# Expert weights in raw pieces of 512 KB: eight pieces in place of four

## The chip, the cores and the metric

One core of one Trainium2 chip runs the program once; the other cores idle. The metric is the device time of that core in microseconds (us). The kernel before was timed in three runs.

## What is computed

The reference is one graph layer on 625 rows of 1024 float32 numbers: a layer norm, a two-step graph convolution and a linear attention, both added to the input, and then a mixture of experts on the normed sum. The change touches only the last part:

```
logits = xf @ router_w; probs = softmax(logits); topw, topi = top_k(probs, 2)      # 8 experts, 2 for each row
h  = silu(xf @ w1[e])        # 1024 x 1024 for each expert
ye = h @ w2[e]               # 1024 x 1024 for each expert
out = x + sum over e of combine[:, e] * ye + sigmoid(xf @ gate_w) * (silu(gate) * up) @ shared_down
```

All weights are float32. The two tables of the 8 experts are 64 MB together.

## The kernel before, in words

**Split products.** TensorE (PE) multiplies in float32r, so every float32 operand is split into a high part (a rounding copy made by ScalarE, ACT) and a low part (raw minus high, made by VectorE, DVE). Products are summed in PSUM from three passes (high x high, high x low, low x high).

**Jobs.** The weights come as a stream of *jobs*, each a half matrix of 1024 x 512 (2 MB). Jobs 0 to 20 are the dense layers, in two loads of 1 MB each; the last of them is J_D = 20, the first half of shared_down. From J_X = 21 on come the experts, four jobs for each: two halves of w1 (called he0 and he1 here) and two halves of w2 (y0 and y1). After the experts, job J_LOOP is the second half of shared_down. An expert job has four *pieces* of 512 KB (PARTS = 4, two of the eight row blocks of 128 each, PK = 2).

**Buffers.** A piece lands in the raw buffer (w_raw, one job's worth: 16 KB per partition), is copied to w_hi and then subtracted into w_lo. w_hi and w_lo are double: job n uses buffer n % 2, so the split of job n waits until PE has finished job n - 2. The raw buffer is single: SyncE's queue (SP, lines 598 to 615) loads piece s of job n once DVE has made w_lo of piece s of job n - 1 (semaphore lo_done). A load therefore runs one half matrix ahead of the split.

**Order on each engine.** The order is written out by hand and is the same for every expert. PE (lines 2260 to 2292): for each of the two halves of w1, two units "he" of 2 x 8 pairs of matmuls (L2274 high weights against both parts of the rows, L2275 low weights against the high part); transposes of the next expert's gathered rows (L1888); then for each of the two halves of w2 one unit "y" for each tile of up to 128 rows, 8 x 3 matmuls (L1842 to L1844) each. The first unit of a job waits for lo_done piece by piece (weights_in, L1851), the others don't wait for weights. ACT (L1030 to 1066): split_hi of the next job, the activation of two "he" units (copy L1039, silu L1041, he_hi L1043), the same for the second half, then xe (L761), split_hi, y_s (L1055, the copy of a y unit out of PSUM) and its store to DRAM (L1063), split_hi, y_s. DVE (L1762 to 1781) has the counterpart: split_lo (L1092), additions L1772, he_lo L1775, xe L1104.

**Experts.** Seven experts have blocks of fixed size, taken in the order of the sizes 208, 128, 208, 128, 152, 152, 152 rows (called e0 to e6 here); they are unrolled. What is left over goes in blocks of 224 rows through a loop with a register count, which makes one pass in this profile (called e7). On SP the experts and the loop are one loop of "every" passes. GpSimd (POOL, L694 to 723) gathers the rows of the next expert into xg by indirect DMA as soon as the present ones are transposed and split.

**Memory.** Region R1's upper half holds in turn part (the normed rows), gate_s (the silu of the shared gate, read for the last time by L1660, which raises prod_done 8 times), and behind it xg; at the end y_first. Region R2 holds xe and he in high and low parts with a row pitch BS of 256, then y_s and he_s. The tail (L731 to 735, L1789 to 1825) gathers each row's two expert rows, scales them and adds, beside the second half of the shared product on PE.

The lines that set the raw buffer's use before are:

```
raw_part = lambda s: w_raw[s // 2][:, s % 2 * PK:(s % 2 + 1) * PK, :]
sp.wait_ge(lo_done, j * (4 * PARTS) + (count_at(J_X + i, s) - PARTS))     # SP: the piece's split of the job before
act.wait_ge(part_loaded[s], by(16 * (job - J_X + 1), base, 64))           # ACT: this piece has landed
```

Of the kernel before, what the change touches and what calls it, by code (L numbers as in the profile page):

```python
# [5 lines left out]
def gps_layer(nc, x, src, dst, w_self0, w_neigh0, b0, w_self1, w_neigh1, b1,  # L6
# [18 lines left out]
    f32, f32r, f16, b16 = mybir.dt.float32, mybir.dt.float32r, mybir.dt.float16, mybir.dt.bfloat16  # L25
    i32, u32 = mybir.dt.int32, mybir.dt.uint32
    ALU, ACT, AX = mybir.AluOpType, mybir.ActivationFunctionType, mybir.AxisListType


    N, D = x.shape  # L30
# [6 lines left out]
    KF = D // 128  # L37
    HW = D // 2
    HK = KF // 2
    TP, TQ = 628, 640  # L40
# [3 lines left out]
    HH = HW // DH  # L44
    X = router_w.shape[1]
    XP = X + 2
    B, BS = 224, 256
    BROWS = (128, B - 128)
    BC = len(BROWS)
    CAPS = (208, 208, 152, 152, 152, 128, 128)  # L50
    ORDER = (1, 7, 2, 6, 3, 4, 5)
    FIXED = len(ORDER)
# [44 lines left out]
    G, U, Dn = halves(gate), halves(up), halves(down)  # L97
# [71 lines left out]
    LOOP = FIXED  # L169
# [25 lines left out]
    PARTS = 4  # L195
# [28 lines left out]
    with ctx:  # L224
# [3 lines left out]
        def at(name, offset, shape, dt):  # L228
            return nc.alloc_sbuf_tensor_at(name, shape, dt, offset=BASE + offset)
# [23 lines left out]
        x1 = at("x1", R1, [T, NT, D], f32)  # L253
        part = at("part", R1 + R1S // 2, [T, NT, D], f32)
        gate_s = at("gate_s", R1 + R1S // 2, [128, HK, TP], f32)
        xg = at("xg", R1 + R1S // 2 + HK * TP * 4, [128, BC, D], f32)

        TAIL = R2 + RGS
        k_tok = at("k_tok", R2, [T, NT, D], f32)
# [17 lines left out]
        he_lo = at("he_lo", R2 + 3 * XE, [128, KF, BS], f32r)  # L277
        y_s = at("y_s", R2 + 4 * XE, [128, 2, HW], f32)
        he_s = at("he_s", R2 + 4 * XE + 2 * HW * 4, [128, 2, 2, B], f32)
        assert 4 * XE + 2 * HW * 4 + 4 * B * 4 <= PAIR  # L280

        c_f = at("c_f", RC, [T, NT, TP], f32)
        c_lo = at("c_lo", RC, [T, NT, TP], f32r)
# [128 lines left out]
        idx2 = following("idx2", [128, BC], u32, 4)  # L412
        table = following("table", [1, 2, FIXED + MAXB], i32, 4)
        assert BASE + off[0] <= nc.sbuf_usable_end, (BASE + off[0], nc.sbuf_usable_end)
        raw_part = lambda s: w_raw[s // 2][:, s % 2 * PK:(s % 2 + 1) * PK, :]
        off = [o_route]
        lgT = following("lgT", [2 * XP, TP], f32, 4)
        lg = following("lg", [T, NT, XP], f32, 4)
# [44 lines left out]
        ready = [sem(f"psum_ready{n}") for n in range(RING)]  # L463
        free = [sem(f"psum_free{n}") for n in range(RING)]
        w_loaded = [sem(f"w_loaded{n}") for n in range(2)]
        part_loaded = [sem(f"part_loaded{n}") for n in range(PARTS)]
        hi_done = sem("hi_done")
        lo_done = sem("lo_done")
        first_hi_done, first_lo_done, half_normal = sem("first_hi_done"), sem("first_lo_done"), sem("half_normal")
# [76 lines left out]
        def _(sp):  # L546
# [51 lines left out]
                load(job, STREAM[job])  # L598


            sp.wait_ge(table_ready, 1)
            every = sp.value_load(table[0:1, 1, 1:2], min_val=X, max_val=FIXED + MAXB - 1)
            sp.wait_ge(lo_done, count_at(J_D, 1))
            with sp.Fori(0, every) as j:
                expert = sp.value_load(table[0:1, 0, bass.ds(j, 1)], min_val=0, max_val=X - 1)
                for i in range(4):
                    for s in range(PARTS):
                        sp.wait_ge(lo_done, j * (4 * PARTS) + (count_at(J_X + i, s) - PARTS))
                        view = (w1v if i < 2 else w2v)[:, bass.ds(expert, 1), s * PK:(s + 1) * PK,
                                                       (i % 2) * HW:(i % 2 + 1) * HW]  # L610
                        sp.dma_start(raw_part(s), view.rearrange("p e k n -> p (e k) n")).then_inc(part_loaded[s], 16)

            for s in range(PARTS):
                sp.wait_ge(lo_done, every * (4 * PARTS) + (count_at(J_X, s) - PARTS))
                sp.dma_start(raw_part(s), Dn[1][:, s * PK:(s + 1) * PK, :]).then_inc(part_loaded[s], 16)
            for n, (i, c0, c1) in enumerate(OUT_PARTS):
                sp.wait_ge(out_ready, n + 1)
                p0, p1 = row_pieces(i)[0]
# [120 lines left out]
        def _(act):  # L739
# [5 lines left out]
            def split_hi(job, base=None, quarters=(0, 1)):  # L745

                b = job % 2
                if job >= 2:
                    wait_unit(last_unit[job - 2], base)
                if job >= J_X:  # L750
                    for s in range(PARTS):
                        act.wait_ge(part_loaded[s], by(16 * (job - J_X + 1), base, 64))
                        copy(w_hi[b][:, s * PK:(s + 1) * PK, :], raw_part(s)).then_inc(hi_done, 1)  # L753
                    return
                for s in quarters:
                    act.wait_ge(w_loaded[s], 16 * (job + 1))
                    copy(w_hi[b][:, s * HK:(s + 1) * HK, :], w_raw[s][:, :, :]).then_inc(hi_done, 1)  # L757
# [324 lines left out]
        def _(dve):  # L1082
            V_ = nc.vector

            def split_lo(job, base=None, quarters=(0, 1)):

                b = job % 2
                if job >= J_X:
                    for s in range(PARTS):
                        dve.wait_ge(hi_done, by(count_at(job, s), base, 4 * PARTS))  # L1090
                        k = slice(s * PK, (s + 1) * PK)
                        V_.tensor_tensor(w_lo[b][:, k, :], raw_part(s), as32(w_hi[b][:, k, :]),  # L1092
                                         ALU.subtract).then_inc(lo_done, 1)
                    return
                for s in quarters:
                    dve.wait_ge(hi_done, count_at(job, s))
                    k = slice(s * HK, (s + 1) * HK)
                    V_.tensor_tensor(w_lo[b][:, k, :], w_raw[s][:, :, :], as32(w_hi[b][:, k, :]),  # L1098
                                     ALU.subtract).then_inc(lo_done, 1)
# [632 lines left out]
            V_.tensor_scalar(table[0:1, 0, 0:FIXED], expert_q[0:1, 0:FIXED], float(X), None, ALU.add)  # L1732
            V_.tensor_scalar(table[0:1, 0, FIXED:FIXED + MAXB], je[0:1, :], float(X - 1), None, ALU.min)
            V_.tensor_copy(table[0:1, 1, 0:1], cum[0:1, 1, X - 1:X])
            V_.tensor_scalar(table[0:1, 1, 1:2], cum[0:1, 1, X - 1:X], float(FIXED), None, ALU.add)
            V_.drain().then_inc(table_ready, 1)
            for h in range(2):
                if h:
# [597 lines left out]
```

## Time and profile before

| | us |
|---|---|
| three runs | 1077.35, 1079.18, 1077.21 (median 1077.35) |
| the profiled execution, its own time | 1080.3 |
| its span (first to last instruction) | 1078.5 |
| PE busy in it | 1052.9 (98%) |
| DVE, ACT, POOL busy | 637.5, 475.1, 75.2 |
| mean granted clock of PE | 0.992 of full |

The profiled execution took 2.95 us longer than the median of the three runs. Times in the rows are counted from the span's start. A row of the timeline has start, duration, engine, line, operation, and in brackets how long the engine was idle before it and what it was waiting for. A matmul's duration is longer than its spacing, because matmuls overlap: PE's progress is read from the starts. The clock is 1.00 at 2.4 GHz and 0.50 at 1.2 GHz; a mean between them is a stretch with both.

### The profile page before, as it was taken

What the parts mean: (1) busy time and instruction counts of PE and PEld (TensorE: products, weight loads), DVE (VectorE), ACT (ScalarE), POOL (GpSimd) and SP (SyncE); (2) the same over time, 40 slices, a digit from 0 to 9 for tenths busy, and PEclk for the clock granted to TensorE, in tenths of its full rate; (3) what the DMA queues carried; (4) which work ended last, traced back from release to release, by engine and by line L of the source; (5) the groups of instructions that cost most, each with busy time, mean ns of one, the idle gap of its engine ahead of it and who ended that gap; (6) DMA issues with size and microseconds to landing.
All of it is one profiled execution on the core that took longest, in us unless ns stands there. A gap on an engine that the chain in (4) does not pass through costs nothing.

```text
span 1078.5 us, 16212 instructions
## 1 busy us (share of the span) xinstructions
PE 1052.9 (98%) x6128; PEld 909.6 (84%) x6128; DVE 637.5 (59%) x963; ACT 475.1 (44%) x771; POOL 75.2 (7%) x123
## 2 busy tenths in 40 slices
PE   7999999999999999999999999999989989999998
PEld 5889998787778999878888999989868878877877
DVE  6789967756656764333275551346566566656546
ACT  4513354547788312211222522126566666647540
POOL 5000010000000000000000072001001000000003
PEclk9999999999999999999999999999989989999999
DMA  9722112123321022630203433225885786777737
GB/s 353 289 79 79 40 40 79 42 87 119 124 79 52 28 79 78 208 141 1 78 1 105 149 79 111 79 98 185 270 287 206 257 293 219 248 248 241 240 123 290
DMA packets 76692, 156.42 MB, mean 145 GB/s; under 512 B 8489, under 2 KB 8987, under 8 KB 76618
## 3 DMA queue, kind: packets, MB, share of 16 engines
q1 hardware_dynamic: 65656, 127.30, 34.5%
q0 software_dynamic: 6416, 20.00, 5.2%
q10 hardware_dynamic: 4546, 8.10, 2.0%
q8 instruction: 49, 0.80, 0.3%
q14 instruction: 25, 0.20, 0.1%
HBM read 133.89 MB, written 21.49 MB: 144 GB/s over the span
## 4 chain that ended last, share of the span: by engine, by line
PE 76%; DVE 8%; DMA 6%; ACT 5%; DVEq 2%; issue 1%; POOL 1%; POOLq 0%; ACTq 0%; SPq 0%
PE ps L1842 20%; PE ps L1844 19%; PE ps L1843 19%; PE ps L2274 5%; DMA w_raw<-in_L_ffn_w 4%; DVE w_lo L1092 4%; PE ps L2275 2%; PE ps L1941 1%; PE ps L2173 1%; PE ps L2104 1%; ACT w_hi L753 1%; PE ps L2174 1%; PE ps L2105 1%; PE ps L1955 1%; DMA y_second<-expert_rows,slots 1%
## 5 line engine op out<-in xcount | busy, mean ns | idle before, releaser
L1092 DVE TENSOR_TENSOR w_lo<-w_raw,w_hi 128x1024 fp32r<-128x1024 f32 x132 | 155.0, 1222 | 80.0 <-ACT w_hi L753 77.6
L753 ACT CAST w_hi<-w_raw 128x1024 fp32r<-128x1024 f32 x132 | 131.3, 1051 | 49.8 <-DMA w_raw<-in_L_ffn_w 24.3
L2274 PE MATMUL ps<-xe,w_hi 128*128 128x304 f32 (+3 forms) x512 | 143.3, 362 | 8.6 <-DVE w_lo L1092 7.7
L2275 PE MATMUL ps<-xe,w_lo 128*128 128x152 f32 (+3 forms) x512 | 125.4, 245 | 0.0
L1098 DVE TENSOR_TENSOR w_lo<-w_raw,w_hi 128x2048 fp32r<-128x2048 f32 x41 | 93.1, 2289 | 38.3 <-ACT w_hi L757 36.2
L2274 PEld LDWEIGHTS ps<-xe,w_hi 128*128 128x128 f32 x512 | 99.6, 194 | 12.8 <-DVE w_lo L1092 8.8
L2275 PEld LDWEIGHTS ps<-xe,w_lo 128*128 128x128 f32 x512 | 101.3, 198 | 0.2
L1842 PE MATMUL ps<-w_hi,xt_hi 128*128 128x512 f32 (+1 forms) x240 | 96.0, 400 | 3.6 <-DVEq L1408 2.0
L757 ACT CAST w_hi<-w_raw 128x2048 fp32r<-128x2048 f32 x41 | 77.1, 1907 | 45.0 <-PE ps L2174 36.2
L1844 PE MATMUL ps<-w_hi,xt_lo 128*128 128x512 f32 (+1 forms) x240 | 93.7, 390 | 0.0
L1843 PE MATMUL ps<-w_lo,xt_hi 128*128 128x512 f32 (+1 forms) x240 | 93.5, 390 | 0.0
L1842 PE MATMUL ps<-w_hi,he_hi 128*128 128x512 f32 (+3 forms) x224 | 89.0, 397 | 2.1 <-DVEq L1773 2.1
L1843 PE MATMUL ps<-w_lo,he_hi 128*128 128x512 f32 (+3 forms) x224 | 87.7, 392 | 0.0
L1844 PE MATMUL ps<-w_hi,he_lo 128*128 128x512 f32 (+3 forms) x224 | 87.7, 392 | 0.0
L1842 PE MATMUL ps<-xt_hi,w_hi 128*128 128x314 f32 x256 | 79.4, 310 | 0.0
L1843 PE MATMUL ps<-t_lo,w_hi 128*128 128x314 f32 x256 | 78.8, 308 | 0.0
L1842 PE MATMUL ps<-t_hi,w_hi 128*128 128x314 f32 x256 | 78.8, 308 | 0.0
L1844 PE MATMUL ps<-xt_hi,w_lo 128*128 128x314 f32 x256 | 78.7, 307 | 0.0
L1844 PE MATMUL ps<-t_hi,w_lo 128*128 128x314 f32 x256 | 78.7, 307 | 0.0
L1843 PE MATMUL ps<-xt_lo,w_hi 128*128 128x314 f32 x256 | 78.6, 307 | 0.0
L871 ACT ACTIVATE src_oh<-iota_c,src_f 128x128 f16<-128x128 bf16 x196 | 62.4, 389 | 20.2 <-DVE o_s L1475 15.6
L1842 PE MATMUL ps<-w_hi,t_hi 128*128 128x512 f32 (+1 forms) x160 | 62.6, 391 | 0.0
(353 smaller groups left out, 2081.1 us busy)
## 6 DMA issues: line engine op xcount, KB each, us to landing
w_raw<-in_L_ffn_w SPq DMA_DIRECT2D x128, 512.0 KB, 3.8
w_raw<-in_L_gnn_W_neigh SPq DMA_DIRECT2D x8, 1024.0 KB, 5.2
w_raw<-in_L_gnn_W_self SPq DMA_DIRECT2D x8, 1024.0 KB, 5.0
w_raw<-in_L_ffn_shared_gate_up SPq DMA_DIRECT2D x8, 1024.0 KB, 6.0
expert_rows<-ctx_s POOLq DMA_DIRECT2D x15, 512.0 KB, 13.7
w_raw<-in_L_mix_Wv SPq DMA_DIRECT2D x4, 1024.0 KB, 13.1
w_raw<-in_L_mix_Wk SPq DMA_DIRECT2D x4, 1024.0 KB, 5.0
w_raw<-in_L_mix_Wq SPq DMA_DIRECT2D x4, 1024.0 KB, 5.2
```

Of the source, the lines that this page charges most:

```text
L753: copy(w_hi[b][:, s * PK:(s + 1) * PK, :], raw_part(s)).then_inc(hi_done, 1)
L757: copy(w_hi[b][:, s * HK:(s + 1) * HK, :], w_raw[s][:, :, :]).then_inc(hi_done, 1)
L871: nc.scalar.activation(src_oh[b][:, c, :], iota_c[:, 0:128, 0], ACT.Abs, bias=src_f[:, g * GC + c:g * GC + c + 1]).then_inc(src_abs, 1)
L1092: V_.tensor_tensor(w_lo[b][:, k, :], raw_part(s), as32(w_hi[b][:, k, :]), ALU.subtract).then_inc(lo_done, 1)
L1098: V_.tensor_tensor(w_lo[b][:, k, :], w_raw[s][:, :, :], as32(w_hi[b][:, k, :]), ALU.subtract).then_inc(lo_done, 1)
L1842: mat(out_ap, lh, rh, start=start, stop=False)
L1843: mat(out_ap, lh, rl, start=False, stop=False)
L1844: return mat(out_ap, ll, rh, start=False, stop=stop)
L1941: last = mat(PB(key)[:, 0:LC], by_place[u % 2][0:rows, n // IL * 128:(n // IL + 1) * 128, n % IL], by_column[u % 2][0:rows, n // IL * LC:( ...
L1955: last = mat(PS(key)[:, a, 0:TD], src_oh[b][:, a * CG + c, :], dst_oh[b][:, a * TD:(a + 1) * TD, c], start=c == 0, stop=c == CG - 1)
L2274: mat(PS(key)[:, a, 0:2 * width], wh[:, k, w_cols], xe[:, :, k, 0:width], start=k == 0, stop=False)
L2275: last = mat(PS(key)[:, a, 0:width], wl[:, k, w_cols], xe_hi[:, k, 0:width], start=False, stop=k == KF - 1)
```

## The change

Expert jobs of odd count (he1 and y1) get a raw buffer of their own, late_raw, four pieces of 512 KB: three lie in the upper half of R1 at its start, where gate_s was, and one at the end of R2. To make room, xg moves up from byte 10048 to byte 12288 of the upper half, the pitch BS of xe and he goes from 256 to 224 (he_s still follows y_s, with a new assertion). Piece s of job n now waits for the split of piece s of job n - 2. The first jobs are exceptions: job J_X waits for the half of J_D that lies in the same bytes, job J_X + 1 for the eighth prod_done. part_loaded becomes two sets of semaphores, one for each parity. SP's one loop over all experts is unrolled for the seven fixed ones, and a loop stays for the blocks; DVE's instruction L1735, which computed the loop's count, goes.

```diff
-    B, BS = 224, 256
+    B, BS = 224, 224
...
-        xg = at("xg", R1 + R1S // 2 + HK * TP * 4, [128, BC, D], f32)
+        PART = PK * HW * 4
+        xg = at("xg", R1 + R1S // 2 + 3 * PART, [128, BC, D], f32)
+        assert HK * TP * 4 <= 3 * PART and 3 * PART + BC * D * 4 <= R1S // 2
...
-        assert 4 * XE + 2 * HW * 4 + 4 * B * 4 <= PAIR
+        R2_PART = 4 * XE + 4 * HW * 4
+        assert 4 * B * 4 <= 2 * HW * 4 and R2_PART + PART <= PAIR
...
-        raw_part = lambda s: w_raw[s // 2][:, s % 2 * PK:(s % 2 + 1) * PK, :]
+        late_raw = [at(f"w_late{s}", R2 + R2_PART if s == 3 else R1 + R1S // 2 + s * PART, [128, PK, HW], f32) for s in range(PARTS)]
+        raw_part = lambda job, s: (late_raw[s][:, :, :] if (job - J_X) % 2 else w_raw[s // 2][:, s % 2 * PK:(s % 2 + 1) * PK, :])
...
-        part_loaded = [sem(f"part_loaded{n}") for n in range(PARTS)]
+        part_loaded = [[sem(f"part_loaded{n}_{s}") for s in range(PARTS)] for n in range(2)]
...
-            sp.wait_ge(table_ready, 1)
-            every = sp.value_load(table[0:1, 1, 1:2], min_val=X, max_val=FIXED + MAXB - 1)
-            sp.wait_ge(lo_done, count_at(J_D, 1))
-            with sp.Fori(0, every) as j:
-                expert = sp.value_load(table[0:1, 0, bass.ds(j, 1)], min_val=0, max_val=X - 1)
+            def load_expert(q, expert, j=None):
+
                 for i in range(4):
+                    job = J_X + 4 * q + i
                     for s in range(PARTS):
-                        sp.wait_ge(lo_done, j * (4 * PARTS) + (count_at(J_X + i, s) - PARTS))
+                        if job == J_X:
+                            sp.wait_ge(lo_done, count_at(J_D, s // 2))
+                        elif job == J_X + 1:
+                            sp.wait_ge(prod_done, KF)
+                        else:
+                            sp.wait_ge(lo_done, by(count_at(job - 2, s), j, 4 * PARTS))
...
-                        sp.dma_start(raw_part(s), view.rearrange("p e k n -> p (e k) n")).then_inc(part_loaded[s], 16)
+                        sp.dma_start(raw_part(job, s), view.rearrange("p e k n -> p (e k) n")).then_inc(part_loaded[i % 2][s], 16)
+
+            sp.wait_ge(table_ready, 1)
+            for q in range(FIXED):
+                load_expert(q, sp.value_load(table[0:1, 0, q:q + 1], min_val=0, max_val=X - 1))
+            blocks = sp.value_load(table[0:1, 1, 0:1], min_val=1, max_val=MAXB - 1)
+            with sp.Fori(0, blocks) as j:
+                load_expert(LOOP, sp.value_load(table[0:1, 0, bass.ds(j + FIXED, 1)], min_val=0, max_val=X - 1), j)
 
             for s in range(PARTS):
-                sp.wait_ge(lo_done, every * (4 * PARTS) + (count_at(J_X, s) - PARTS))
-                sp.dma_start(raw_part(s), Dn[1][:, s * PK:(s + 1) * PK, :]).then_inc(part_loaded[s], 16)
+                sp.wait_ge(lo_done, blocks * (4 * PARTS) + count_at(J_LOOP - 2, s))
+                sp.dma_start(raw_part(J_LOOP, s), Dn[1][:, s * PK:(s + 1) * PK, :]).then_inc(part_loaded[0][s], 16)
...
-                        act.wait_ge(part_loaded[s], by(16 * (job - J_X + 1), base, 64))
-                        copy(w_hi[b][:, s * PK:(s + 1) * PK, :], raw_part(s)).then_inc(hi_done, 1)
+                        act.wait_ge(part_loaded[(job - J_X) % 2][s], by(16 * ((job - J_X) // 2 + 1), base, 32))
+                        copy(w_hi[b][:, s * PK:(s + 1) * PK, :], raw_part(job, s)).then_inc(hi_done, 1)
...
-                        V_.tensor_tensor(w_lo[b][:, k, :], raw_part(s), as32(w_hi[b][:, k, :]),
+                        V_.tensor_tensor(w_lo[b][:, k, :], raw_part(job, s), as32(w_hi[b][:, k, :]),
...
-            V_.tensor_scalar(table[0:1, 1, 1:2], cum[0:1, 1, X - 1:X], float(FIXED), None, ALU.add)
```

## Rows read from the trace of the kernel before

**Rows 1.** Windows of e1, e2 and e4: PE, PEld, DVE, ACT, POOL busy, clock, DMA share, GB/s.
```profile
767.90:796.30 28.40, 27.58 (x193) 25.01 (x191) 20.30 (x25) 20.03 (x31) 0.94 (x1) 1.00 0.71 236
796.30:846.20 49.90, 45.90 (x234) 38.78 (x235) 28.79 (x30) 28.32 (x37) 3.85 (x2) 0.93 0.76 261
...
874.00:914.00 40.00, 35.39 (x206) 29.90 (x206) 24.29 (x29) 24.22 (x36) 2.20 (x3) 0.87 0.74 259
```

**Rows 2.** Waits of 740 to 1050 us: who waited for whom: total, times, longest.
```profile
ACT y_s L1055 <- PE ps L1844: 48.4, 15, 5.0
...
ACT w_hi L753 <- DMA w_raw<-in_L_ffn_w: 24.3, 28, 2.0
```

**Rows 3.** Timeline of PE, the start of e2 and of e4, with the waits.
```profile
796.86 0.43 PE L2274 MATMUL ps<-xe,w_hi 128*128 128x416 f32 x1 [0.58 <-DVE w_lo L1092]
...
797.22 0.36 PE L2274 MATMUL ps<-xe,w_hi 128*128 128x416 f32 x1
...
799.82 0.45 PE L2274 MATMUL ps<-xe,w_hi 128*128 128x416 f32 x1 [2.14 <-DVE w_lo L1092]
...
803.24 0.72 PE L2274 MATMUL ps<-xe,w_hi 128*128 128x416 f32 x1 [0.81 <-DVE w_lo L1092]
...
874.90 0.38 PE L2274 MATMUL ps<-xe,w_hi 128*128 128x304 f32 x1 [0.84 <-issue]
...
881.79 0.62 PE L2274 MATMUL ps<-xe,w_hi 128*128 128x304 f32 x1 [1.60 <-DVE w_lo L1092]
```

**Rows 4.** Timeline of ACT ahead of e2 and of e4.
```profile
792.97 0.76 ACT L761 CAST xe<-ps 128x320 fp32r<-128x320 f32 x2 [0.78 <-ACT y_s L1055]
794.40 1.05 ACT L753 CAST w_hi<-w_raw 128x1024 fp32r<-128x1024 f32 x1 [0.68 <-DMA w_raw<-in_L_ffn_w]
...
870.23 0.38 ACT L761 CAST xe<-ps 128x96 fp32r<-128x96 f32 x2 [0.48 <-ACT y_s L1055]
```

**Rows 5.** Timeline of DVE ahead of e2 and of e4.
```profile
789.14 4.63 DVE L1092 TENSOR_TENSOR w_lo<-w_raw,w_hi 128x1024 fp32r<-128x1024 f32 x4
793.69 1.12 DVE L1104 TENSOR_TENSOR xe<-ps,xe 128x320 fp32r<-128x320 f32 x2
...
871.25 0.66 DVE L1104 TENSOR_TENSOR xe<-ps,xe 128x96 fp32r<-128x96 f32 x2
```

**Rows 6.** Windows at the last stall of e2, of e4, and the stall of e2.
```profile
803.24:810.00 6.76, 6.76 (x29) 6.62 (x30) 3.67 (x3) 3.86 (x5) 0.00 (x0) 0.63 0.88 308
881.79:889.00 7.21, 7.21 (x39) 7.21 (x40) 5.29 (x5) 4.41 (x6) 0.00 (x0) 0.66 0.92 316
795.90:803.30 7.40, 3.38 (x15) 2.12 (x13) 4.49 (x4) 3.95 (x5) 0.12 (x1) 0.87 1.00 363
```

**Rows 7.** Timeline of PE: first w2 matmul of e1, e3, e5 and e6.
```profile
784.47 0.50 PE L1842 MATMUL ps<-w_hi,he_hi 128*128 128x512 f32 x1 [0.80 <-DVEq L1773]
...
862.03 0.50 PE L1842 MATMUL ps<-w_hi,he_hi 128*128 128x512 f32 x1 [0.18 <-DVEq L1773]
...
939.01 0.48 PE L1842 MATMUL ps<-w_hi,he_hi 128*128 128x512 f32 x1
...
979.92 0.50 PE L1842 MATMUL ps<-w_hi,he_hi 128*128 128x512 f32 x1 [1.12 <-DVEq L1773]
```

**Rows 8.** The issues of L611 (count, duration in ns), and the DMA queue of 750 to 1050 us.
```profile
L611 SPq DMA_DIRECT2D w_raw<-in_L_ffn_w x128: 372/373/697, 677.4 to 1021.0; - x128
...
DMA to landing us min/median/max: 3.5/3.8/7.6
...
q1 hardware_dynamic: 31552, 60.82, 59.4%
```

**Rows 9.** Timeline of SP: the four loads of e2's first job.
```profile
790.55 3.76 SPq L611 DMA_DIRECT2D w_raw<-in_L_ffn_w  x4
```

**Rows 10.** Groups of instructions by line (the page): busy us, mean ns, idle before.
```profile
L1842 PE MATMUL ps<-w_hi,xt_hi 128*128 128x512 f32 (+1 forms) x240 | 96.0, 400 | 3.6 <-DVEq L1408 2.0
...
L1842 PE MATMUL ps<-w_hi,he_hi 128*128 128x512 f32 (+3 forms) x224 | 89.0, 397 | 2.1 <-DVEq L1773 2.1
```

## The prediction

> **What bounds the kernel now.** I read the page first: PE is busy for 98% of the span, so at most about 25 us of idle time and what the clock lost can be won. Then the windows of the experts [rows 1]. They show where both lie: e2 and e4 have 4.0 and 4.6 us without PE work and a mean clock of 0.93 and 0.87; e1 has 0.8 us and a full clock. Nothing outside the experts is touched. Then the waits [rows 2]: ACT waited 28 times, 24.3 us in all, for a raw piece. It only hurts where PE is near behind, and the timeline of PE shows where [rows 3]: e2's first unit waits for w_lo before each of its four pieces, the last time until 803.24; e4's does until 881.79. Both follow an expert of 128 rows, the shortest work per byte of weights. The reason is in the load's trigger: the four loads of e2's first job are issued from 790.55 to 794.3 [rows 9], as DVE makes w_lo of the job before [rows 5], and take 3.5 to 7.6 us to land [rows 8]. ACT is ready for the first piece at 793.7, after the xe copies [rows 4], and the DMA share is 1.00 with 363 GB/s just then [rows 6].
>
> **The change, part by part.**
>
> *Loads two halves ahead.* e2's first job is issued when e1's first w2 job is split, some 9 to 10 us earlier (one job of PE work: e1's 28.4 us over four jobs is 7.1 on average [rows 1], and more where he units lie between). Then ACT finds its pieces, and its own pace and DVE's decide. I replay both places with durations of the rows. A series of four w_lo takes 4.63: 1.22 to the first and 1.14 for each further one [rows 5]. For e2: ACT ends xe at 793.73 and makes the first w_hi in 1.05 [rows 4], until 794.8; DVE ends its xe at 794.81 [rows 5]. So w_lo are ready at 796.1, 797.3, 798.4 and 799.55. PE, which would have begun at 796.28 (796.86 less 0.58), works through the two pairs of a piece in less than DVE's 1.14 (two pairs begin within 0.36 [rows 3], so some 0.6), and waits still for the second, third and fourth piece, 0.5 us or a little more each. The last wait ends at 799.57 and not at 803.24: **3.67 us**.
>
> For e4: ACT ends xe at 870.61, w_hi is ready at 871.7, DVE is free at 871.91, w_lo are ready at 873.2, 874.3, 875.45 and 876.6. PE would begin at 874.06 [rows 3], waits for the last two pieces, 0.5 and 0.6, and is through at 876.60 and not at 881.79: **5.19 us**.
>
> *The clock.* After these last waits the clock was still at 1.2 GHz for a while. A window of length t with mean clock c costs t x (1 - c): 6.76 x 0.37 = **2.50** and 7.21 x 0.34 = **2.45** [rows 6]. Where PE waited once for 1.12 us (e6 [rows 7]) the clock did not fall. The waits that I leave sum to about 1.7 and 1.1 us, nearer to that than to the 4.0 and 4.6 before which it fell, so I take both terms.
>
> The Trainium skill (TensorE: Matmul & The Clock Gate, HAM oscillation) puts such a fall down to one long wait for a load, after which the work starts cold. By that rule a series of short waits would cost nothing, and the sum would be the same with no doubt on these terms. The trace differs: its longest wait before either fall is 2.14 us [rows 3], and it is the series that did it. The measurement decides, so a fall is kept as a rival.
>
> *Two smaller stalls.* The first w2 matmul waits for the PSUM buffer that DVE frees behind a w_lo series: 0.80 us in e1, 0.18 in e3 of the same shape, 1.12 in e6, none in e5 of the same shape [rows 7]. In e1 and e6 the job before had waited for its pieces. With them there I take e3's and e5's values: **0.62** and **1.12**.
>
> *What costs.* (a) SP's loop is unrolled; an issue takes 0.37 us and at most 0.70 [rows 8], and SP is a job ahead, so new code costs it nothing that shows; without that cover one slow issue is 0.3 us. (b) J_X + 1's loads stand behind the wait for prod_done on SP, and J_X + 2's behind them. prod_done's last comes before DVE starts on J_X's split, which released the same loads before: earlier, nothing lost. (c) The pitch of 224 in place of 256 and xg's new place change addresses and no instruction. No row shows two pitches of one tile; the nearest are the matmuls on he at pitch 256 and those on xt at 640, with means of 397 and 400 ns [rows 10]. I take 0, between -0.5 and +0.5. (d) The loop's head on SP comes once less for each fixed expert and once at e7: 0. Before, it stood ahead of every expert's first load, and e2's was issued 0.19 us after the w_lo that released it (789.14 + 1.22 to 790.55 [rows 5, 9]), which is its bound. (e) L1735 works on one element, long before PE's first expert: 0. (f) y_s stores and gathers meet the same bytes, spread more evenly: 0; the bound is a rival below. (g) The tail is released by the last y unit and moves with PE as it is: 0.
>
> **Sum.** 3.67 + 5.19 + 2.50 + 2.45 + 0.62 + 1.12 = 15.55 us. Against the profiled execution's 1080.3 that is 1064.75. The median of the runs is 2.95 lower, so I expect 1061.8, say **1062**. The 2.95 may be a fall of the clock that the other runs had not (one costs 2.5); then the gain on the median is nearer to 13, and the result 1064.
>
> **The rivals.**
>
> *The clock falls all the same* at one or both places, because a series of three short waits is enough. For it: the kind of wait is the same. Against: half its length or less. It gives 2.5 or 5.0 more: 1064.5 to 1067. 0.15.
>
> *The DMA rate is the bound.* In e1, 8.39 MB of weights, 0.85 MB of gathered rows (208 of 4 KB) and 0.52 MB of stores are 9.8 MB. The weight queue moved 60.82 MB in 59.4% of 300 us, 341 GB/s [rows 8]; 9.8 MB then take 28.6 us, while PE needs 27.6 [rows 1]. So the short experts eat 1 us of lead each. The new lead is 2.1 MB, or 6.1 us, and the experts of 208 rows fill it again (e2 moves 261 GB/s at 0.76). If a second bound (a gather in between, as at 795) eats it all the same, about half of the 8.9 us stays and the clock falls: 1062 + 4.4 + 5.0 = 1071. 0.12.
>
> *It doesn't do what it says.* If some wait in SP's fixed order holds the early loads back to where they were, the time is that of before, 1077. I find none: all of n - 2's waits have long been passed. 0.04.
>
> *Slower: the stores of y.* Each y_s copy waits on ACT for the store of the same tile one half before, and the next w_hi stand behind it. If twice as many weights are queued ahead of a store, it lands 4 pieces x 1.54 us = 6.2 later. It decides once a store takes more than the 5.5 us between halves in an expert of 128 rows (e3's two from 862.03 to 874.06 [rows 3, 7], transposes left out). Two experts of 128 rows and three of 152 would lose up to 6.2 and 2.5 of clock each, 8.7: with two of them 1062 + 17.4 = 1079.4, with three 1088. Against: in the trace all 15 waits ahead of y_s were for PE and none for a store [rows 2], though the DMA share was at 1.00 [rows 6], and a piece is still issued only when a piece is used up. 0.05, at 1083. The Trainium skill (DMA: Bandwidth & Descriptors, Queues, rings and completion order) has each DMA engine take turns between queues; by that a store doesn't stand behind the weights' backlog at all. No row separates the two.
>
> **How the numbers follow.** Forecast 0.62 (1060 to 1065), clock 0.15, rate 0.12, no change 0.04, slower 0.05, else 0.02. The range: at the lower end the forecast with the 2.8 us of waits that I leave gone and the pitch's 0.5, 1058.5; at the upper end the rate rival, 1071. About 0.1 lies outside, mostly above. A measurement here can tell about 0.2%, 2.2 us, from no change; faster by more 0.91, within 0.04, slower 0.05.
>
> **What the profile would show.** Right: ACT's waits for raw pieces fall from 24.3 us to a few, none ahead of e2 and e4; PE waits three times for w_lo by 0.5 to 0.7 in e2 and twice in e4; clock 1.00 in both; L611's issues for an expert's first job a job earlier; DMA share lower in e2's and e4's first 8 us. Wrong: ACT still waiting for pieces at those places (rate), short waits with a clock below 1 (clock), ACT waiting for expert_rows ahead of y_s (slower), or a new wait of PE for xe, whose rows now have the weights beside them in the DMA queues.

## The result, and the profile after

| | before | after |
|---|---|---|
| median of the runs, us | 1077.28 (4 runs, 1075.98 to 1079.18) | 1066.17 (4 runs, 1065.63 to 1067.30) |
| the profiled execution: own time, span | 1080.3, 1078.5 | 1065.63, 1063.5 |
| mean granted clock | 0.992 | 1.000 |

The ratio is 0.9892, 95% interval 0.9879 to 0.9906: 11.6 us faster by the ratio (11.1 by the medians), clear of noise. The forecast was 1062, in a range of 1058.5 to 1071.

The two profiled executions are 15.0 us apart in their spans, where the sum said 15.55. Of the 15.0, 14.1 lie ahead of PE's last matmul and 0.9 behind it, in the work that follows it to the end of the span: 4.8 us before, 4.0 after, and 4.0 to 5.8 over the twelve traces of this document, so the 0.9 need not be the change's.

```profile
1073.64 0.28 PE L1844 MATMUL ps<-w_hi,s_lo 128*113 128x256 f32 x1
...
1059.56 0.28 PE L1857 MATMUL ps<-w_hi,s_lo 128*113 128x256 f32 x1
```

The medians are 11.1 apart. So the replay was nearly right for the execution that it was made on, and the step from that execution to the median was not; both are taken up below.

Windows of the kernel after, over e1, e2 and e4 as in [rows 1] (columns: PE, PEld, DVE, ACT, POOL busy, clock, DMA share, GB/s), and over the eight experts:

```profile
767.90:795.70 27.80, 27.54 (x194) 24.97 (x192) 20.62 (x26) 21.25 (x33) 1.28 (x1) 1.00 0.66 231
795.70:839.60 43.90, 43.10 (x234) 36.18 (x234) 27.56 (x29) 25.96 (x36) 4.49 (x3) 1.00 0.84 293
867.60:899.50 31.90, 31.10 (x202) 25.96 (x201) 21.79 (x27) 20.33 (x33) 3.83 (x4) 1.00 0.90 330
735.00:1035.00 300.00, 297.86 (x1759) 246.64 (x1759) 187.75 (x214) 186.53 (x273) 19.90 (x17) 1.00 0.69 240
```

e2 has 0.8 us without PE work in place of 4.0, and the clock is 1.00 throughout. The waits of ACT and PE over 735 to 1035 us:

```profile
ACT y_s L1069 <- PE ps L1857: 55.9, 18, 5.0
...
ACT y_s L1069 <- DMA expert_rows<-y_s: 1.0, 1, 1.0
...
PE ps L2287 <- DVE w_lo L1106: 1.6, 5, 0.4
PE ps L1855 <- DVEq L1786: 0.5, 2, 0.3
```

ACT's 24.3 us for raw pieces [rows 2] are gone without a rest. What is left of PE's waits stands in its timeline at the start of e2 and of e4, beside [rows 3]:

```profile
796.72 0.45 PE L2287 MATMUL ps<-xe,w_hi 128*128 128x416 f32 x1 [0.23 <-DVE w_lo L1106]
797.85 0.46 PE L2287 MATMUL ps<-xe,w_hi 128*128 128x416 f32 x1 [0.29 <-DVE w_lo L1106]
798.99 0.46 PE L2287 MATMUL ps<-xe,w_hi 128*128 128x416 f32 x1 [0.28 <-DVE w_lo L1106]
...
869.16 0.41 PE L2287 MATMUL ps<-xe,w_hi 128*128 128x304 f32 x1 [0.40 <-DVE w_lo L1106]
...
870.30 0.41 PE L2287 MATMUL ps<-xe,w_hi 128*128 128x304 f32 x1 [0.41 <-DVE w_lo L1106]
```

These idle times are counted from the modelled end of the matmul before. Read by the starts, each against the usual 0.10 us (e2) or 0.07 us (e4) between those two matmuls, the three gaps of e2 cost 1.26 us and the two of e4 1.12. The waits come 1.14 us apart, which is the rhythm of DVE's series ahead of e2. DVE is busy here from 788.48 on with no gap above 0.2 us, where before it stood until 795.49 for a late piece (the last row is of the kernel before):

```profile
788.48 4.63 DVE L1106 TENSOR_TENSOR w_lo<-w_late,w_hi 128x1024 fp32r<-128x1024 f32 x4
793.03 1.12 DVE L1118 TENSOR_TENSOR xe<-ps,xe 128x320 fp32r<-128x320 f32 x2
794.30 4.63 DVE L1106 TENSOR_TENSOR w_lo<-w_raw,w_hi 128x1024 fp32r<-128x1024 f32 x4
...
795.49 1.23 DVE L1092 TENSOR_TENSOR w_lo<-w_raw,w_hi 128x1024 fp32r<-128x1024 f32 x1 [0.68 <-ACT w_hi L753]
```

The trigger, beside [rows 9]: e2's first four loads are issued 10 us earlier, the second four where its first were.

```profile
780.14 3.77 SPq L618 DMA_DIRECT2D w_raw<-in_L_ffn_w  x4
789.87 3.78 SPq L618 DMA_DIRECT2D w_late<-in_L_ffn_w  x4
```

### The profile page after: what moved, and what is told of

Read it like the earlier page. It is cut to its first block, busy times and chain, and to the rows that moved or that the text cites. A ratio compares the mean times of both kernels' runs of the same rounds, so it can differ in the third digit from the quotient of the medians.

```text
span 1063.5 us, 16078 instructions
## 1 busy us (share of the span) xinstructions
PE 1047.4 (98%) x6128; PEld 904.0 (85%) x6128; DVE 635.0 (60%) x962; ACT 472.6 (44%) x771; POOL 78.5 (7%) x123
## 4 chain that ended last, share of the span: by engine, by line
PE 82%; DVE 7%; ACT 4%; DVEq 2%; DMA 2%; issue 1%; POOL 1%; POOLq 0%; ACTq 0%; SPq 0%
PE ps L1855 21%; PE ps L1856 21%; PE ps L1857 21%; PE ps L2287 7%; DVE w_lo L1106 3%; PE ps L2288 3%; PE ps L1954 1%; PE ps L2186 1%; PE ps L2187 1%; PE ps L2117 1%; PE ps L2118 1%; PE ps L1968 1%; PE ps L1901 1%; ACT src_oh L885 1%; DMA y_second<-expert_rows,slots 1%
## 5 line engine op out<-in xcount | busy, mean ns | idle before, releaser
L2287 PE MATMUL ps<-xe,w_hi 128*128 128x304 f32 (+3 forms) x512 | 137.4, 350 | 1.6 <-DVE w_lo L1106 1.6
L2288 PE MATMUL ps<-xe,w_lo 128*128 128x152 f32 (+3 forms) x512 | 123.1, 240 | 0.0
L2287 PEld LDWEIGHTS ps<-xe,w_hi 128*128 128x128 f32 x512 | 96.1, 188 | 4.8 <-DVE w_lo L1106 2.7
L1855 PE MATMUL ps<-w_hi,xt_hi 128*128 128x512 f32 (+1 forms) x240 | 96.0, 400 | 3.6 <-DVEq L1422 2.0
L2288 PEld LDWEIGHTS ps<-xe,w_lo 128*128 128x128 f32 x512 | 97.7, 191 | 0.3
L1106 DVE TENSOR_TENSOR w_lo<-w_raw,w_hi 128x1024 fp32r<-128x1024 f32 x68 | 78.8, 1221 | 31.7 <-ACT w_hi L767 31.3
L1106 DVE TENSOR_TENSOR w_lo<-w_late,w_hi 128x1024 fp32r<-128x1024 f32 x64 | 74.1, 1220 | 36.3 <-ACT w_hi L767 34.9
L1857 PE MATMUL ps<-w_hi,xt_lo 128*128 128x512 f32 (+1 forms) x240 | 93.6, 390 | 0.0
L1855 PE MATMUL ps<-w_hi,he_hi 128*128 128x512 f32 (+3 forms) x224 | 89.3, 399 | 0.5 <-DVEq L1786 0.5
L1857 PE MATMUL ps<-w_hi,he_lo 128*128 128x512 f32 (+3 forms) x224 | 88.1, 394 | 0.0
L1855 PE MATMUL ps<-xt_hi,w_hi 128*128 128x314 f32 x256 | 79.4, 310 | 0.0
L1855 PE MATMUL ps<-t_hi,w_hi 128*128 128x314 f32 x256 | 78.8, 308 | 0.0
L1857 PE MATMUL ps<-xt_hi,w_lo 128*128 128x314 f32 x256 | 78.7, 307 | 0.0
L1857 PE MATMUL ps<-t_hi,w_lo 128*128 128x314 f32 x256 | 78.7, 307 | 0.0
L767 ACT CAST w_hi<-w_late 128x1024 fp32r<-128x1024 f32 x64 | 62.4, 1051 | 23.1 <-PE ps L1857 18.0
```

Of the source, the lines that this page charges most:

```text
L767: copy(w_hi[b][:, s * PK:(s + 1) * PK, :], raw_part(job, s)).then_inc(hi_done, 1)
L1106: V_.tensor_tensor(w_lo[b][:, k, :], raw_part(job, s), as32(w_hi[b][:, k, :]), ALU.subtract).then_inc(lo_done, 1)
L1855: mat(out_ap, lh, rh, start=start, stop=False)
L1857: return mat(out_ap, ll, rh, start=False, stop=stop)
L2287: mat(PS(key)[:, a, 0:2 * width], wh[:, k, w_cols], xe[:, :, k, 0:width], start=k == 0, stop=False)
L2288: last = mat(PS(key)[:, a, 0:width], wl[:, k, w_cols], xe_hi[:, k, 0:width], start=False, stop=k == KF - 1)
```

## The experiments

Line numbers of PE, ACT and DVE differ by a few between the kernels; L1842 to L1844 of before are L1855 to L1857 after, and L2274 is L2287. Each kernel was timed beside the kernel before on the same chip, in three batches: experiments 1, 2, 4 and 9; 3, 6, 8 and 10; 5 and 7. "PE's last" is the start of the last matmul of the trace.

**1. space_no_lead: all of the change but the lead.**

```diff
-                        elif job == J_X + 1:
-                            sp.wait_ge(prod_done, KF)
                         else:
-                            sp.wait_ge(lo_done, by(count_at(job - 2, s), j, 4 * PARTS))
+                            sp.wait_ge(lo_done, by(count_at(job - 1, s), j, 4 * PARTS))
...
-                sp.wait_ge(lo_done, blocks * (4 * PARTS) + count_at(J_LOOP - 2, s))
+                sp.wait_ge(lo_done, blocks * (4 * PARTS) + count_at(J_LOOP - 1, s))
```

> The changed kernel with its eight pieces, its layout, its unrolled SP queue, but each load triggered one half matrix ahead as before. Theory (the lead alone wins the time): same as the kernel before within 0.2%, with ACT again waiting some 24 us for raw pieces and PE waiting for w_lo in e2 and e4 until a fourth piece. Rival (the gain came from the layout, the unrolled queue or the separate buffers): within 3 us of the changed kernel, 1066. Rival (the layout costs something that the lead has to pay back, which would explain why the gain on the medians is 11 and not 15): 2 to 4 us slower than before.

Measured: 1078.81 (12 runs) against 1076.84 of before (17 runs), ratio 1.0016 (1.0002 to 1.0030). The waits are back:

```profile
PE ps L2285 <- DVE w_lo L1104: 7.6, 6, 2.6
PE ps L1853 <- DVEq L1784: 2.1, 3, 1.0
...
ACT w_hi L765 <- DMA w_raw<-in_L_ffn_w: 13.9, 13, 2.5
ACT w_hi L765 <- DMA w_late<-in_L_ffn_w: 6.7, 10, 1.2
```

So the lead alone wins the time. But the rest of the change has a price of its own, which the forecast had put at nothing. The interval leaves 0.2 to 3.2 us for it; experiment 6 shows what in the change has it.

**2. lead_two_jobs: the lead for the first job of e2 and of e4 only.** The edit is shown against space_no_lead.

```diff
+                            ahead = 2 if q in (2, 4) and i == 0 else 1
-                            sp.wait_ge(lo_done, by(count_at(job - 1, s), j, 4 * PARTS))
+                            sp.wait_ge(lo_done, by(count_at(job - ahead, s), j, 4 * PARTS))
```

> As space_no_lead, but the first job of e2 and of e4 alone is loaded two halves ahead. Theory (only these two places hurt, by 3.7 and 5.2 us of waits and by the clock after them): the clock stays at 1.00, PE's waits there shrink to below 1.5 us each, and of the changed kernel's gain all but the 1.7 us of e1's and e6's small stalls is there: 1066 to 1069. Rival (each load ahead helps a little everywhere): less than half of the gain, 1072 or more. Rival (moving two loads only shifts the wait to the next job, whose pieces are then late): waits for w_lo appear in e2's and e4's second job, 1070 or more.

Measured: 1072.79 (6 runs), ratio 0.9962 (0.9947 to 0.9977). The theory's 1066 to 1069 is missed, and the rival that the wait moves to the next job holds. e2's first job comes in time, and then ACT waits for the second one, which lies in w_late (timeline of ACT):

```profile
793.16 3.90 ACT L766 CAST w_hi<-w_raw 128x1024 fp32r<-128x1024 f32 x4
...
799.97 1.05 ACT L766 CAST w_hi<-w_late 128x1024 fp32r<-128x1024 f32 x1 [2.43 <-DMA w_late<-in_L_ffn_w]
803.07 1.05 ACT L766 CAST w_hi<-w_late 128x1024 fp32r<-128x1024 f32 x1 [2.05 <-DMA w_late<-in_L_ffn_w]
805.94 1.05 ACT L766 CAST w_hi<-w_late 128x1024 fp32r<-128x1024 f32 x1 [1.83 <-DMA w_late<-in_L_ffn_w]
```

From the first he unit to the first w2 product e2 takes 23.86 us here and 21.60 with the full lead, e4 21.88 and 18.02: the 6.1 us that are missing, and in e4 the clock still falls:

```profile
795.80:819.70 23.90, 21.50 (x137) 20.03 (x136) 15.54 (x16) 13.18 (x19) 0.72 (x1) 1.00 0.69 245
870.10:892.00 21.90, 19.53 (x138) 18.57 (x136) 14.25 (x16) 12.13 (x18) 1.95 (x2) 0.92 0.80 269
```

**3. lead_four_jobs: the second jobs too.** The edit is shown against lead_two_jobs.

```diff
-                            ahead = 2 if q in (2, 4) and i == 0 else 1
+                            ahead = 2 if q in (2, 4) and i < 2 else 1
```

> As lead_two_jobs, with the second job of e2 and of e4 two halves ahead as well. With two jobs the stall ahead of e2 and e4 went, but ACT then waited for the second job's pieces (2.4, 2.1, 1.8, 0.3 us) and 6.4 us of the changed kernel's gain were missing. Theory (the wait had moved to the next load, and from the second job on the he units are long enough to take a load one half ahead): 1067.5 to 1069, no waits of ACT for pieces in e2's and e4's second job. Rival (it moves on to the third job, and only a lead at every job holds): still 1071 or more.

Measured: 1066.92 (4 runs, 1066.69 to 1070.04), ratio 0.9904 (0.9889 to 0.9918), where the changed kernel has 0.9901 in its repetition. Four of 32 expert jobs carry the gain in its median, which is even a little below the 1067.5 to 1069 expected, and the rival falls. One sign of the theory did not come: ACT does wait for a piece in the second jobs, 0.56 us in e2 and 1.16 us in e4, but PE's waits for w_lo there are those of the changed kernel (1.6 us). The profiled execution, the slowest of the four, has a wait of 1.19 us ahead of e6's first w2 product. It is in neither trace of the changed kernel, but the trace of lead_two_jobs, where e6's loads don't come earlier either, is also without it: it comes in some executions only. What the other 28 leads bring to the median isn't shown, since the intervals of 1066.92 and 1066.44 overlap almost whole.

**4. after_again: how the runs scatter.** No edit.

> The changed kernel once more, beside the others on the same chip. Theory: 1066, ratio 0.989 to before. What is open is why the profiled executions differ by 14.7 us and the medians by 11: if the kernel before in other executions keeps its clock or loses it for a shorter time, its runs here scatter over several us (1076 to 1080) while this one's stay within 2; if instead the profiled execution of before was an odd one for other reasons, this one's runs scatter as much.

Measured: 1066.44 (5 runs, 1066.16 to 1067.13), ratio 0.9901 (0.9885 to 0.9917). The kernel before ran 17 times beside it: 1074.37 to 1079.34, its clock between 0.990 and 0.994 (in the later batches 0.989 to 0.995), its spans 1072.6 to 1077.6 with a median of 1075.1. The changed kernel's clock was 0.999 or 1.000 in all five. So the profiled execution of before, with a span of 1078.5, lay above all 17 of them (of the 52 runs of that kernel in the three batches, two were longer), and the scatter of 5 us falls to 1 with the stalls. The mean clock explains a part of it only: over the 52 runs it goes with the span (correlation -0.60), with a mean span of 1078.0 at a clock of 0.990 (5 runs) and 1075.2 at 0.994 (18 runs), but the five at 0.992, the clock of the profiled execution, have a mean of 1076.2. All 52 lay between 0.989 and 0.995, so a fall of the clock was in every one.

**5. fill_waits: the price of the clock alone.** The kernel before, with PE kept at work while it waits.

```diff
+            FILL = {(2, 0, 0): 2, (2, 0, 2): 9, (2, 0, 4): 2, (2, 0, 6): 3,
+                    (4, 0, 0): 3, (4, 0, 2): 9, (4, 0, 6): 7}
...
+                                    for _ in range(FILL.get((q, h, k), 0)):
+                                        mat(PS(key)[:, 1, 0:512], s_hi[:, 0, 0:128], s_hi[:, 0, 0:512], start=True, stop=True)
                                     weights_in(job + h, k, j)
```

> The kernel before, with 35 matmuls of 0.23 us that compute nothing, placed ahead of the waits for w_lo in the first unit of e2 and of e4, about as many as fill each wait of the profile (2, 9, 2, 3 and 3, 9, 0, 7). They write a PSUM bank that is started anew afterwards. The pieces come as late as before. Theory (the clock's fall is a cost of its own, caused by PE's waiting): the clock stays at 1.00 through e2 and e4, and it is 2 to 5 us faster than before although it does more work, 1072 to 1075; the stalls themselves stay. Rival (the clock's fall costs nothing of its own, since PE had to wait for pieces anyway): the same time as before or 1 us more, whatever the clock does. Rival (the fill comes too late or too early in most executions): the clock still falls and the time is 0 to 3 us more than before.

Measured: 1074.19 (12 runs) against 1077.63 (17 runs), ratio 0.9970 (0.9956 to 0.9985): 35 matmuls more, and 3.2 us faster. The windows of [rows 6]:

```profile
803.24:810.00 6.76, 6.76 (x47) 6.72 (x46) 4.34 (x4) 4.47 (x5) 0.00 (x0) 1.00 0.92 312
881.79:889.00 7.21, 7.21 (x60) 7.21 (x59) 4.25 (x7) 4.15 (x8) 0.00 (x0) 1.00 0.87 299
```

47 and 60 matmuls fit where 29 and 39 did, at a clock of 1.00 in place of 0.63 and 0.66. The clock's fall is a cost of its own, caused by PE's idling; the theory holds. One of the twelve runs had a mean clock of 0.997 and was the slowest, 1076.95. The kernel's own waits stay: by the ratios to before, 0.9970 and 0.9901, it is 7.4 us behind the changed one.

**6. before_pitch_224: the one number of the layout.** The runs above had shown that each w2 stage with a full tile is 0.1 us longer after the change, wherever the loads come.

```diff
-    B, BS = 224, 256
+    B, BS = 224, 224
```

> The kernel before with one number changed: the row pitch BS of xe and he 224 instead of 256. In the changed kernel each w2 stage with a full tile of 128 rows is 0.1 us longer than before (e3's first 6.36 instead of 6.27), and the kernel with the space but without the lead was 1.6 us slower than before. Theory (the pitch does it: matmuls that take a 128-column tile of he as the stationary operand are spaced 0.232 us and not 0.228): the same 0.1 us per full tile here, 384 such matmuls, 1.7 us in all, 1078.5 if before is 1077. Rival (it was the new place of xg or the raw pieces' place or SP's unrolled code): the spacing stays 0.228 and the time is that of before.

Measured: 1079.49 (12 runs) against 1076.91 (17 runs), ratio 1.0020 (1.0009 to 1.0031): 2.2 us slower, 1.0 to 3.3. The timeline of PE, from e3's first w2 product to the first of its second half (24 products and 8 transposes, no wait between): the kernel before, this one, the changed kernel.

```profile
862.03 0.50 PE L1842 MATMUL ps<-w_hi,he_hi 128*128 128x512 f32 x1 [0.18 <-DVEq L1773]
...
868.30 0.50 PE L1842 MATMUL ps<-w_hi,he_hi 128*128 128x512 f32 x1
```

```profile
862.19 0.50 PE L1842 MATMUL ps<-w_hi,he_hi 128*128 128x512 f32 x1 [0.27 <-DVEq L1773]
...
868.55 0.50 PE L1842 MATMUL ps<-w_hi,he_hi 128*128 128x512 f32 x1
```

```profile
855.59 0.50 PE L1855 MATMUL ps<-w_hi,he_hi 128*128 128x512 f32 x1 [0.28 <-DVEq L1786]
...
861.96 0.50 PE L1855 MATMUL ps<-w_hi,he_hi 128*128 128x512 f32 x1
```

6.27, 6.36 and 6.37 us. Averaged over the starts within a unit of the w2 products that take a full tile of he as the stationary operand, the spacing is 0.228 us with a pitch of 256 and 0.232 with 224; with the narrower tiles (24, 80, 96 rows) it is 0.230 to 0.234 in both. 384 full products times 0.0044 us are 1.7 us, and the 96 on tiles of 80 rows (0.2335 and 0.2310) give 0.2 back. The theory holds; where xg lies and how SP is written have no part in these 0.1 us. The reported durations moved with the spacing; the kernel before and this one:

```profile
L1842 PE MATMUL ps<-w_hi,he_hi 128*128 128x512 f32 x128 | 50.9, 398 | 2.1 <-DVEq L1773 2.1
...
L1843 PE MATMUL ps<-w_lo,he_hi 128*128 128x512 f32 x128 | 49.9, 390 | 0.0
...
L1842 PE MATMUL ps<-w_hi,he_hi 128*128 128x512 f32 x128 | 51.5, 402 | 1.5 <-DVEq L1773 1.5
...
L1843 PE MATMUL ps<-w_lo,he_hi 128*128 128x512 f32 x128 | 50.3, 393 | 0.0
```

**7. before_pitch_240.** As above with 240.

> The kernel before with a row pitch of 240 numbers (960 bytes) in xe and he. With 256 (1024 bytes) the w2 products on a full tile of 128 rows are spaced 0.2279 us on average, with 224 (896 bytes) 0.2323; the tiles of 80, 96 and 24 rows, which begin 512 bytes into the pitch of 1024, had 0.230 to 0.234 with either. Theory A (the spacing is short only where the stationary tile begins on a multiple of 1024 bytes from the region's start): 240 is as slow as 224, 0.232, e3's unit 6.36 us. Theory B (it is the particular pitch of 896): 240 is as quick as 256, 0.228, e3's unit 6.27 us. One look only; the time is read from the spacing.

Measured: e3's unit took 6.36 us (860.71 to 867.07), the spacing 0.231. So 224 is not peculiar: the 256, 1024 bytes, is the quick one of the three. Theory A holds for he, but not as a rule on multiples of 1024 bytes: on xt, with a pitch of 2560 bytes, the same average over the kernel before gives 0.227 to 0.228. What of the address decides was not settled. The times (1076.29 beside 1076.48) are of one run each and tell nothing about 2 us, since the runs of the kernel before spread over 3.7 to 7.4 us in each batch.

```profile
860.71 0.51 PE L1842 MATMUL ps<-w_hi,he_hi 128*128 128x512 f32 x1 [0.31 <-DVEq L1773]
...
867.07 0.50 PE L1842 MATMUL ps<-w_hi,he_hi 128*128 128x512 f32 x1
```

**8. pitch_256: the change without its layout price.** The fourth late piece goes to the routing's scratch.

```diff
-    B, BS = 224, 224
+    B, BS = 224, 256
...
-        late_raw = [at(f"w_late{s}", R2 + R2_PART if s == 3 else R1 + R1S // 2 + s * PART, [128, PK, HW], f32) for s in range(PARTS)]
+        late_raw = [at(f"w_late{s}", o_route if s == 3 else R1 + R1S // 2 + s * PART, [128, PK, HW], f32) for s in range(PARTS)]
...
                             sp.wait_ge(prod_done, KF)
+                            sp.wait_ge(zero_stored, 16)
```

> The changed kernel with the pitch of 256 kept; the fourth late piece lies in the routing's scratch instead of at the end of R2, and its loads wait for the zeroing of the slot table too, long past. Theory (pitch): w2 stages as before, 1.5 to 1.9 us less than the changed kernel, 1064.6. Rival (pitch is nothing): within 0.5 us of the changed kernel, 1066.3.

Measured: 1064.87 (4 runs), ratio 0.9884 (0.9870 to 0.9898). e3's unit is 6.28 us again, and PE's last starts at 1058.27, after 1059.56 in the changed kernel: 1.3 us, a little less than the 1.5 expected. The intervals of the two kernels' times overlap; it is the profile that shows the step.

```profile
855.35 0.49 PE L1856 MATMUL ps<-w_hi,he_hi 128*128 128x512 f32 x1 [0.18 <-DVEq L1787]
...
861.63 0.50 PE L1856 MATMUL ps<-w_hi,he_hi 128*128 128x512 f32 x1
```

**9. high_first: the waits that the forecast left.** In the first he unit of a half, the 16 products with high weights come first.

```diff
+                        if n == h * HK // 2:
+                            for a in range(2):
+                                for k in range(KF):
+                                    if a == 0 and k % PK == 0:
+                                        pe.wait_ge(hi_done, by(count_at(job + h, k // PK), j, 4 * PARTS))
+                                    mat(PS(key)[:, a, 0:2 * width], wh[:, k, cols[a]], xe[:, :, k, 0:width], start=k == 0, stop=False)
+                            for a in range(2):
+                                for k in range(KF):
+                                    if a == 0:
+                                        weights_in(job + h, k, j)
+                                    last = mat(PS(key)[:, a, 0:width], wl[:, k, cols[a]], xe_hi[:, k, 0:width], start=False,
+                                               stop=k == KF - 1)
...
```

> The changed kernel, but in the first he unit of each half matrix PE does all 16 products with the high weights first (waiting for the high copies only) and the 16 with the low weights after them. Theory (the waits that are left in e2 and e4, 1.6 us, come from DVE's rhythm of 1.14 us for each w_lo while PE is through a piece in half of that): they vanish, the high products begin about 1 us sooner, and it is 1.5 to 2 us faster than the changed kernel, 1064 to 1065. Rival (the waits then turn up before the first w2 product, for the PSUM buffer or he_lo, since ACT and DVE are no faster): within 0.5 us of the changed kernel.

Measured: 1063.95 (5 runs, 1063.49 to 1065.09), 2.5 us under after_again in the same batch, whose lowest run is 1066.16, and a little more than the 1.5 to 2 expected. Timeline of PE at e2's start, without a wait:

```profile
795.94 3.40 PE L2288 MATMUL ps<-xe,w_hi 128*128 128x416 f32 x16
799.18 1.93 PE L2293 MATMUL ps<-xe,w_lo 128*128 128x208 f32 x16
```

By the time PE comes to the low weights (799.18) DVE has made all four (a series of 4.63 us from 794.58). From the first he unit to the first w2 product e2 takes 20.21 us instead of 21.60 and e4 16.86 instead of 18.02, about the 1.26 and 1.12 us that the gaps cost by the starts. PE's first w2 product waits no longer than before (0.6 us in two places, against 0.5), so the rival falls.

**10. pitch_256_high_first: both.** The two edits above together.

> Both of the earlier steps in one: the pitch of 256 and the high products first. Theory (they are independent: one is matmul spacing in w2, the other waits in w1): 2.4 plus 1.7 us below the changed kernel, 1062.3. Rival (the shorter w2 stages only give PE more time to wait for w_lo, which DVE's rhythm sets): no better than high_first alone, 1064.

Measured: 1062.96 (4 runs, 1062.75 to 1063.65), ratio 0.9870 (0.9855 to 0.9884), 1.3% faster than before and the fastest of all. PE's last starts at 1056.31, after 1057.44 with high_first alone: the pitch gives 1.1 us here, against 1.3 alone, and the two edits add up nearly whole; the time is 0.7 us above the 1062.3 expected.

## Why the prediction was right, and where it was off

**The place and the mechanism** were right: ACT's waits for pieces went from 24.3 us to none, the clock stayed up, and the loads ahead of e2 moved by 10 us (said: 9 to 10). Experiment 1 shows that nothing else in the change does it. Experiments 2 and 3 show that the lead of the first two jobs of e2 and e4 is what counts.

**The replay**, against the profiled execution. w_lo of e2 was to start 0.66 us (the shift by then) before 794.9, and started at 794.30. The last wait in e2 was to end at 799.57, less the 0.7 that had been won by then, and ended at 798.99. By PE's starts, from the first product of the second w2 half of the expert before to the first w2 product of e2 and e4 themselves, 33.27 us became 27.27 and 31.12 became 23.70: 6.00 and 7.42, where 6.17 and 7.64 were said. The waits that I left cost 1.26 and 1.12 us by the starts, where 1.7 and 1.1 were said (the 0.8 us of idle time in each is another measure, as said above). e1's small stall gave 0.62 as said, e6's stretch 1.37 for 1.12. Together that is 15.41 us; PE's last matmul moved by 14.1, and the difference fits what the w2 stages lost by the pitch.

**The clock** was to fall no more, for 4.95 us. It fell nowhere, and experiment 5 puts a price on it by itself: 3.2 us (1.6 to 4.7) in the mean of the runs, with the extra work included. That a series of waits is enough, against the one long wait of the Trainium skill (TensorE: Matmul & The Clock Gate, HAM oscillation), is borne out: filling the series kept the clock up. In lead_two_jobs PE's waits in e4 summed to 2.3 us, none above 0.9, and the clock's mean was still 0.92. Waits of 0.8 in e2 and e4 after the change made no fall, and neither did 1.66 us in two waits (0.58 and 1.08) that fill_waits left in e4. What of a series decides is not shown.

**The step that failed is (c)**: "No row shows two pitches of one tile; ... I take 0, between -0.5 and +0.5." It measures 1.3 us (experiment 8, in the trace) to 2.2 (experiment 6, in the runs, interval 1.0 to 3.3). The comparison that it rested on, 397 and 400 ns [rows 10], was of two tiles and of groups with several forms: it could not tell what another pitch does to he. Once one tile stands at two pitches, the durations show it (398 and 402 ns, 390 and 393 in experiment 6) as the starts do. The bound of 0.5 us had no row under it for 384 matmuls: 3 ns on each of them are 1.2 us already.

**The second miss is the step to the median.** I subtracted what one execution would lose from the median of others. That execution's span was 3.4 us above the median span of the 17 runs of experiment 4 (1075.1), and the span of the one after was 0.9 below its repetition's median (1064.4): 15.0 less these two is 10.7, near the 11.1 of the medians. The doubt was named ("the result 1064"), but it was not put into the forecast, and the reason given for it, a fall of the clock that other runs had not, was wrong: every one of the 52 later runs had one. Other traces of kernels whose loads run one half ahead show where it lay. The stretches of e2 and e4 that took 33.27 and 31.12 us in the execution of the replay took 31.59 and 29.77 in before_pitch_240, whose span was 1074.5. In space_no_lead and before_pitch_224, whose profiled executions had long spans too (1080.2 and 1081.2), they took 34.08 and 30.95, 33.33 and 32.88. e6's stretch took 18.12 us in the execution of the replay, 17.33 in before_pitch_224 and 16.77 in before_pitch_240, where the changed kernel has 16.75. And e1's stall of 0.80 us, ahead of all that fill_waits changes, is 0.17 in its trace:

```profile
783.85 0.50 PE L1842 MATMUL ps<-w_hi,he_hi 128*128 128x512 f32 x1 [0.17 <-DVEq L1773]
```

So the terms of the sum were read right, but from an execution with a long span, and a stall that costs 1 us in one execution is missing from another. With 15.55 less about 1.5 for the pitch and 2.95 for the unusual execution, 11.1 us remain, the difference of the medians. This agreement is partly luck, since the terms are uncertain by 0.5 us and more.

**The rivals.** *Clock:* no. *DMA rate:* the engines are as busy in e2 and e4 after the change as before, which I had forecast otherwise ("DMA share lower in e2's and e4's first 8 us"). The share is 0.96 and 1.03, where the same stretches before have 0.97 to 1.00 and 1.03, by windows of the changed kernel:

```profile
795.67:803.00 7.33, 6.53 (x40) 5.76 (x40) 7.25 (x7) 6.09 (x8) 0.68 (x1) 1.00 0.96 333
867.64:875.00 7.36, 6.56 (x50) 6.20 (x49) 6.42 (x7) 5.12 (x7) 1.94 (x2) 1.00 1.03 376
```

What runs there now are loads that nobody waits for yet. The lead was enough for ACT to wait for no piece. *It doesn't do what it says:* no. *Slower by the stores of y:* its mechanism is in the trace, without an effect that shows in the changed kernel. ACT waited once for a store, 0.98 us ahead of a y_s copy in e4, where the trace of before has no such wait; in lead_four_jobs it was 2.7 us in two places, PE's waits in that stretch (790 to 895) were 2.6 us in all against 1.9 in the changed kernel, and e4 took 19.02 us to its first w2 product against 18.02. I do not know how much of that is the stores'; ACT waited 1.16 us for a piece there too. Whether a store stands behind the weights' backlog stays open.

## What to carry to other kernels

A double buffer whose load starts when the buffer is emptied covers the load by one stage's work only; where stage lengths vary, size the lead by the shortest pair of stages, and look for the next load in the queue, since a lead at one place moves the wait to the next one. Look for what the room for the buffer costs: here the tighter rows took back an eighth of the gain, and another corner of memory had the space. Before subtracting a trace's stalls from a median, see how the kernel's own runs scatter: here the stalls and the falls of the clock behind them varied from run to run, and went with the change. And where PE waits for a two-step preparation, issue first what needs only the first step.

## What the runs showed of the hardware

- The spacing of float32r matmuls of 512 columns depends on the pitch of the stationary tile: 0.228 us at 1024 bytes, 0.231 at 960, 0.232 at 896 (he, 128 columns). The mean reported durations moved alike, 390, 393 and 393 ns for L1843. On a tile of 80 columns 1024 bytes is the slower one, 0.2335 against 0.2310 at 896.
- Idling of 4.0 and 4.6 us in pieces of 2.14 us or less went with a fall of the clock to 1.2 GHz, and 35 empty matmuls in its place kept the clock at 1.00 and saved 3.2 us.
- With the loads two halves ahead, pieces take longer to land, a median of 5.3 us against 3.8, and ACT waits for none of them. The issues of the expert's loads in the kernel after (compare [rows 8], 3.5/3.8/7.6):

```profile
L618 SPq DMA_DIRECT2D w_late<-in_L_ffn_w x64: 372/373/373, 697.3 to 996.5; - x64
...
DMA to landing us min/median/max: 3.5/5.3/10.3
```
